# A perceiver block on one core: the matrix work of its first self-attention in another order

## The reference

```python
x = x + cross_attention(ctx_1024, layernorm(x), ...)
x = x + attn(layernorm(x), q_weight, v_weight, out_w, out_b)
x = x + moe_attention(layernorm(x), ...)

def attn(x, q_weight, v_weight, out_w, out_b):     # t = 8, b = 64, 16 heads of 32
    q = einsum('tbm,mhd->tbhd', x, q_weight)
    q_sq = einsum('tbhd,tbhd->tbh', q, q)
    squared_dist = q_sq[:, None] + q_sq[None, :] - 2.0 * einsum('tbhd,sbhd->tsbh', q, q)
    attn_weights = softmax(-squared_dist * inv_sqrt_d, axis=1)
    A = einsum('mhd,nhd->hmn', q_weight, q_weight) * inv_sqrt_d
    XA = einsum('tbm,hmn->tbhn', x, A)
    PXA = einsum('tsbh,sbhm->tbhm', attn_weights, XA)
    PXAV = einsum('tbhm,mhd->tbhd', PXA, v_weight).reshape(...)
    return PXAV @ out_w.T + out_b
```

## Time and profile before

| | us |
|---|---|
| median of 3 runs | 582.81 |
| lowest and highest | 582.78 to 582.81 |
| the profiled execution, whole time | 586.54 |
| its span, first to last instruction | 584.8 |
| TensorE busy in the span | 570.4 |
| VectorE, ScalarE, GpSimd busy | 344.6, 203.7, 222.4 |
| mean granted TensorE clock | 0.991 |

### The profile page before, as it was taken

The page is one execution under the profiler, slowest core; times in us unless marked ns, Lnnn a source line. Parts: engine busy times, 40 slices in busy tenths (PEclk is TensorE's granted clock), DMA queues, the critical chain, the costliest instruction groups (busy, mean ns, idle before and its releaser), DMA issues.

```text
span 584.8 us, 11726 instructions
## 1 busy us (share of the span) xinstructions
PE 570.4 (98%) x5010; PEld 489.0 (84%) x5010; DVE 344.6 (59%) x387; ACT 203.7 (35%) x293; POOL 222.4 (38%) x182
## 2 busy tenths in 40 slices
PE   6999999999999999999999999999999999999997
PEld 6989889898989989897678988988888888788886
DVE  4886871825637082552597446656666345876741
ACT  4444342505335250532652530423342121434320
POOL 2599685564627356461325000202434443000000
PEclk9999999999999999999999978999999999999999
DMA  8764424240322324005210402013923322799701
GB/s 304 280 222 149 154 75 153 72 153 29 114 81 75 149 72 153 1 1 158 61 68 3 154 4 72 17 57 111 245 86 86 130 73 73 156 220 240 176 1 72
DMA packets 25284, 65.76 MB, mean 112 GB/s; under 512 B 2424, under 2 KB 2424, under 8 KB 22304
## 3 DMA queue, kind: packets, MB, share of 16 engines
q1 hardware_dynamic: 25248, 65.23, 36.6%
HBM read 64.05 MB, written 1.18 MB: 112 GB/s over the span
## 4 chain that ended last, share of the span: by engine, by line
PE 90%; DVE 5%; issue 2%; ACT 1%; POOL 1%; DMA 1%; ACTq 0%; DVEq 0%
PE ps L328 17%; PE ps L330 17%; PE ps L329 17%; PE ps L849 10%; PE ps L872 4%; PE ps L876 4%; PE ps L864 2%; PE ps L859 2%; PE ps L863 2%; PE ps L858 2%; PE ps L1148 2%; PE ps L929 1%; PE ps L890 1%; PE ps L897 1%; DVE stats L1358 1%
## 5 line engine op out<-in xcount | busy, mean ns | idle before, releaser
L466 POOL TENSOR_TENSOR psum_tmp<-psum_tmp,raw 128x512 f32<-128x512 f32 (+1 forms) x88 | 140.8, 1600 | 29.4 <-DVE lo L1385 20.7
L849 PE MATMUL ps<-hi 128*128 128x256 f32 (+3 forms) x416 | 130.1, 314 | 5.5 <-ACT hi L543 4.8
L849 PEld LDWEIGHTS ps<-hi 128*128 128x128 f32 (+1 forms) x416 | 79.1, 190 | 6.3 <-ACT hi L543 4.8
L328 PE MATMUL ps<-hi,gh 128*128 128x512 f32 x192 | 75.6, 394 | 1.2 <-DVE gl L1768 1.2
L1385 DVE TENSOR_TENSOR lo<-raw,hi 128x2048 fp32r<-128x2048 f32 (+1 forms) x29 | 63.3, 2215 | 21.4 <-ACT hi L535 21.4
L330 PE MATMUL ps<-hi,gl 128*128 128x512 f32 x192 | 74.8, 390 | 0.0
L329 PE MATMUL ps<-lo,gh 128*128 128x512 f32 x192 | 74.7, 389 | 0.0
L516 POOL TENSOR_TENSOR sx<-sx,raw 128x512 f32<-128x512 f32 x32 | 41.1, 1289 | 78.1 <-DVE raw L1734 78.1
L735 ACT ACTIVATE hi<-raw 128x2048 fp32r<-128x2048 f32 x14 | 26.8, 1917 | 85.5 <-PE ps L330 76.5
L328 PE MATMUL ps<-wvh,gh 128*128 128x512 f32 x128 | 51.1, 399 | 0.2 <-DVE gl L1541 0.2
L330 PE MATMUL ps<-wvh,gl 128*128 128x512 f32 x128 | 50.0, 391 | 0.0
(11 more groups left out here) (224 smaller groups left out, 1177.7 us busy)
## 6 DMA issues: line engine op xcount, KB each, us to landing
raw<-in_ctx SPq DMA_DIRECT2D x23, 1024.0 KB, 4.8
raw<-in_ve SPq DMA_DIRECT2D x8, 1024.0 KB, 5.5
raw<-in_oe SPq DMA_DIRECT2D x8, 1024.0 KB, 7.6
wk<-gm_rows SPq DMA_DIRECT2D x8, 512.0 KB, 9.8
g<-gm_rows SPq DMA_DIRECT2D x8, 512.0 KB, 10.4
raw<-in_ctx SPq DMA_DIRECT2D x8, 130.0 KB
xres<-in_x SPq DMA_DIRECT2D x1, 1024.0 KB, 9.8
mb<-in_WqT SPq DMA_DIRECT2D x1, 1024.0 KB, 13.4
```

The source lines that it names most:

```text
L328: pe.matmul(dst, wh, xh, start=first, stop=False)
L466: pool.tensor_tensor(psum_tmp[0:k, :], (raw[:, 0, :] if t == 1 else psum_tmp[0:k, :]), raw[0:k, t, :], ALU.add).then_inc(ctx_sum, 1)
L849: pe.matmul(dst, hi[0:kk, t, cols], x, start=start and opens, stop=stop and closes, skip_group_check=True)
```

## The change

Nothing is added to the computation or taken from it. The same matmuls, copies and exponentials run in another order, in three PSUM places and partly on another engine:

- TensorE: `half_norms(0)` and `half_norms(1)` come one query block earlier. The fourth query block, `project_1(1, (3,))`, moves from ahead of `distances(0)` to behind it. `distances(1)` moves ahead of `head_values(2)`. `near_values(0)` and `near_values(1)` are cut in two: the halves for groups 0 and 1 stand between `head_values(2)` and `head_values(3)`, the others behind it. `near_values(2)` moves ahead of the first transposes, and `near_values(3)` ahead of all of the projection. The projection finishes tile 0, then 1, 2 and 3, where before the first halves of the tiles 0, 1 and 2 came first.
- Waits: a half of `near_values` waits for the values of its own groups. The wait for the second row terms stands at `near_values(0)` instead of `head_values(3)`, and `head_values(3)` waits for two `vv_done`.
- ScalarE copies out all four groups of values. `w_high(W_Q2, 0, 2)` moves ahead of the third copy, and the split of the gate weights (L704) ahead of `near_high(0)`.
- VectorE: no `values_out`. `near_add(3)` and `w_low(W_Q2, 0)` come ahead of `near_norm(0)`, `near_norm(2)` ahead of `near_low(0)`, and the low part of the gate weights ahead of `near_norm(3)`.
- PSUM: `vv_bank(3)` is bank 7 instead of 0, `num_bank` of the blocks 2 and 3 are exchanged, and `turn_bank` alternates between the banks 0 and 3.

The two copies of values have left VectorE, and the weight split stands ahead of the first division. The diff, cut to what the order doesn't show:

```diff
         def vv_bank(g):
-            return bank[(6, 7, 3, 0)[g]]
+            return bank[(6, 7, 3, 7)[g]]
...
         def num_bank(c, g):
-            return ((0, 3), (6, 7), (1, 2), (4, 5))[c][g // 2]
+            return ((0, 3), (6, 7), (4, 5), (1, 2))[c][g // 2]
...
         def turn_bank(c):
-            return bank[(0, 3, 1, 2)[c]]
+            return bank[3 * (c % 2)]
...
             values_out(1)
+            w_high(W_Q2, 0, 2)
+            values_out(2)
             nearness(2)
             nearness(3)
-            near_high(0)
-            near_high(1)
-            w_high(W_Q2, 0, 2)
+            values_out(3)
...
-                if g >= 2:
-                    pe.wait_ge(row_done, g - 1)
+                if g == 2:
+                    pe.wait_ge(row_done, 1)
+                if g == 3:
+                    pe.wait_ge(vv_done, 2)
...
-            def near_values(c):
+            def near_values(c, gs=range(NG)):
                 pe.wait_ge(d_exp, c + 1)
                 if c == 0:
                     pe.wait_ge(vv_ones, 1)
-                    pe.wait_ge(vv_done, NG)
+                    pe.wait_ge(row_done, 2)
                 if c == 2:
                     pe.wait_ge(d_add, 8)
-                for g in range(NG):
+                for g in gs:
+                    pe.wait_ge(vv_done, g + 1 if c != 1 or g < 2 else NG)
...
             pe.wait_ge(w_lo, 4)
-            near_values(2)
             out_part(0, (0, 1))
-            near_values(3)
-            out_part(1, (0, 1))
             turn_values(2)
             turn_values(3)
-            out_part(2, (0, 1))
-            for i in range(3):
-                out_part(i, (2, 3))
+            out_part(1, (0, 1))
+            out_part(0, (2, 3))
+            out_part(1, (2, 3))
+            out_part(2, range(KC))
             out_part(3, range(KC))
```

More of the change, by code:

```diff
@@ L704, in _ @@
             act.activation(wg_hi, wg_raw, ACT.Copy).then_inc(wg_hi_done, 1)
+            near_high(0)
+            near_high(1)
             near_high(2)
@@ L1096, in _ @@
             transposes_1(3)
-            project_1(1, range(3))
+            project_1(1, range(2))
             half_norms(0)
-            project_1(1, range(3, KC))
+            project_1(1, range(2, 3))
             half_norms(1)
@@ L1150, in near_values @@
                                            vv[row, g, 4 * c + j, :], start=True, stop=True, skip_group_check=True)
-                mm.then_inc(nv_mm, 1)
+                if gs.stop == NG:
+                    mm.then_inc(nv_mm, 1)
             def turn_values(c):
@@ L1161, in _ @@
             distances(0)
+            project_1(1, range(3, KC))
+            half_norms(2)
             head_values(0)
-            half_norms(2)
+            half_norms(3)
             head_values(1)
-            half_norms(3)
+            distances(1)
             head_values(2)
+            near_values(0, range(0, 2))
+            near_values(1, range(0, 2))
             head_values(3)
-            distances(1)
-            near_values(0)
-            near_values(1)
+            near_values(0, range(2, NG))
+            near_values(1, range(2, NG))
+            near_values(2)
             turn_values(0)
             turn_values(1)
+            near_values(3)
             def transpose_e(u):
@@ L1612, in near_add @@
                                       row, ALU.add).then_inc(d_add, 1)
[L1614 to L1618, removed]
             def near_norm(c):
@@ L1637, in _ @@
             row_part(1)
-            values_out(2)
-            values_out(3)
             near_add(2)
+            near_add(3)
+            w_low(W_Q2, 0)
             near_norm(0)
-            near_add(3)
             near_norm(1)
+            near_norm(2)
             near_low(0)
             near_low(1)
-            near_norm(2)
-            w_low(W_Q2, 0)
-            near_norm(3)
             dve.wait_ge(wg_hi_done, 2)
             dve.tensor_tensor(wg_lo, wg_raw, wg_hi.bitcast(F32), ALU.subtract).then_inc(wg_lo_done, 1)
+            near_norm(3)
             near_low(2)
```

## The result

| | before | changed |
|---|---|---|
| median of 20 runs, us | 586.64 | 582.17 |
| lowest to highest | 581.85 to 591.16 | 580.26 to 583.79 |
| ratio to before, 95% interval | | 0.994 (0.9914 to 0.9965) |
| profiled execution, whole and span | 586.54, 584.8 | 580.85, 579.1 |
| mean granted clock of it, as a share of full speed | 0.991 | 1.000 |

The changed kernel is faster by 0.6%. The ratio leaves out runs of a kernel more than 1.5% above its fastest, here four of before (590.8 to 591.2), so it lies nearer to one than the quotient of the two medians, 0.992. The time landed within the predicted range and 0.8 us from the predicted one, but from another base than the one that I used: the three runs of before that were shown (582.8) lay near the lower end of what that kernel does. Between the medians of 20 runs lie 4.5 us, not 1.4.

The account below looks back on a forecast made before the run. TensorE, busy 98% of the span, was taken as the bound. Terms +0.3 + 0.2 - 0.4 - 0.3 - 1.2 = -1.4 us from the median 582.81 give 581.4; likeliest 580.6 to 582.4, whole range 578.0 to 583.9.

Parts of the forecast that it names:

- the fall is the profiled execution's own: Rival: median runs have no clock fall, only waits and tail gain, -0.2 us, 582.6; chance 0.22 including equal loss.
- The clock: TensorE's sparse run from 342.2: fall at start of block 3's products, 3.3 us lost instead of 4.49, -1.2 us.
- the rival of the longer fall: Clock falls at about 344.5, before block 2's products, and stays low into the projection: 5.7 lost, 583.8; chance 0.14.
- Clock stays up: Rival: head values among the products prevent the fall, all of 4.49 us comes back, -4.7, 578.1; chance 0.17.
- Before the first head values: TensorE waits 0.5 us for ScalarE's square of the fourth query block, replacing a 0.22 stall: +0.3, bounds 0 and +0.5.
- The copy of group 3: Block 0's later products: TensorE waits for ScalarE's copy of group 3's values, +0.2 us, bounds 0 to +1.1.
- The second turns: Block 2's products hide the second division, so the 0.43 us wait for VectorE goes: -0.4, up to -0.7.
- The gap before the queries: Next layer's queries: tiles in order free VectorE sooner, gap about 0.7 instead of 0.94 us; -0.3, bounds -0.5 and 0.
- Stalls put down to issue: TensorE durations carried over from the kernel before, among them 3.14 us for the second distances.

Follow-up runs that it names:

- head values together: Changed kernel with the last two blocks of head values together ahead of all value products, these no longer in halves; high-clock median 581.22 us, the others 586.8 to 590.0.
- fourth block first with early turn: Changed kernel with the fourth query block back ahead of the first distances and the next layer's first transposes ahead of the last six projection matmuls; median 580.44 us, ratio 0.9899.
- the kernel with extra matmuls: Kernel before with eight extra 512-column matmuls between the value products of blocks 0 and 1; median of all runs 584.72 us, high-clock median 584.68.
- the tiles in order: Kernel before with only the projection finishing the token tiles in order; high-clock median 583.75 us, the others 586.6 to 591.5.
- block 2 ahead: Kernel before with only block 2's value products moved ahead of the first transposes; high-clock median 583.27 us, the others 585.7 to 592.4.
- extra transposes: Kernel before with 24 extra 128 by 128 transposes between the value products of blocks 0 and 1; high-clock median 584.41 us, the others 586.1 to 588.4.
- turns last: Changed kernel with block 3's value products directly behind block 2's, ahead of the first transposes; median 581.84 us, all 12 runs at high clock.
- third heads first: Changed kernel with the third block of head values ahead of the second distances, as before; high-clock median 581.01 us, the others 583.8 to 584.3.

## Why the prediction held, and where it didn't

**The base.** I subtracted 1.4 us from a median of three runs and arrived at 581.4; measured were 582.17. The three runs agreed within 0.03 us, and I took that for the kernel's spread. It was not: the kernel before has a spread of 9 us, by the clock. My rival "the fall is the profiled execution's own" came near the truth and stopped short of it: those three were presumably executions without a fall (582.8, as the high ones' 582.2), the profiled one had a fall, and over many runs half or more have one. The forecast of the time was right by luck: the base was 3.8 us too low and the gain 3.1 us too small, and the two nearly cancel. Of the change it held the direction and a third of the size.

**The clock.** This is the step that failed. I let the fall come at the start of block 3's products and replaced the 4.49 us of before by 3.3, -1.2, where the profile gives back all of the 4.49. The changed kernel's profile has none, and its runs have rare falls of 0.996 to 0.997. The wrong inference was to measure the sparse stretch from its beginning at 342.2 and carry over the two distances of 4.1 and 7.3 us from one trace. Before, distances and products together stood from 336.8 to 350.7 without head values or projection; in the changed kernel head values stand at 337.4 and at 340.4, and only 7.2 us are left behind them. The fall that I took also counts the first turns ahead of it as part of the sparse stretch; no run shows that transposes weigh in it like products, and with 24 extra ones in it 9 of 12 runs kept the clock, against 9 of 34 without. Nor does a low clock last until the projection in every case, as the rival of the longer fall assumed: it rose at 337.4 (head values together) and at 341.1 (fourth block first with early turn), both in the second distances behind head values. "Clock stays up" had 0.17 and 578.1; from the profiled 586.5 its -4.7 gives 581.8, and 580.85 was measured.

**Waits.** Before the first head values: +0.5 predicted ahead of what it replaced, 0.38 measured. The copy of group 3: +0.2 predicted, 0.21 measured; by the trace ScalarE began it 0.04 behind the head values (341.62 against 341.58), and the weight loads went on 0.05 behind its end (342.27 against 342.22), together the 0.1 that I had estimated for signals. The second turns: wait gone, as predicted, and 0.50 at high clock in the kernel with extra matmuls. The gap before the queries: 0.94 to 0.70, as predicted, and with the tiles alone as well. These four steps were right, within about 0.1 us each. One count in the working is wrong: the rest of blocks 0 and 1 behind the last head values is 64 instructions, not 96; the times given for it are those of 64.

**Stalls put down to issue.** I kept them: I gave the second distances 3.14 us and let the 0.51 among the products stand. In the changed kernel the distances take 2.47 (334.88 to 337.35) and no such stall is left among the products, 1.2 us less than I carried. The waits take off another 0.4 by the traces (+0.16 and +0.21, -0.50 and -0.24). Together that is more than the 0.7 to 1.1 us between the kernels at high clock, and how it divides isn't shown, since no trace of before at high clock is at hand; in other kernels the stall in the distances is 0.17 instead of 0.45. The stalls' cause stays open. The 0.51 stands at the same place in the traces of before, of the tiles in order and of block 2 ahead (after 70 product instructions); extra matmuls between the blocks removed it, extra transposes left 0.21 of it, both left 0.17 in the distances; and ordering the third head values as before did not bring any back.

## What to carry to other kernels

Before pricing a change on a few runs that agree, look at the granted clock of the profile: where it falls once in the middle, the time has a spread that three runs can hide (here 582.78 to 582.81 in the first three, 581.85 to 591.16 in twenty), and the base of the sum may be off by more than the change. Here head values that had to run anyway went into a long stretch of small matmuls, and the clock that stayed up was worth more than the waits that this added (4.5 us in the profiled executions against 0.6); it is the first thing to try where the clock falls in such a stretch. A transpose that feeds another engine can go ahead of the last matmuls of the product before it; here that closed a gap of 0.70 us.

## What the runs showed of the hardware

- The clock can fall in a stretch of small matmuls in which TensorE's gaps are no longer than 0.5 to 0.65 us. Counted from the last head values before it to the next projection matmul, the sparse stretch was 13.8 us in the profiled execution of before (336.8 to 350.7, part of it at low clock; 17 of 35, 25 of 34, 14 of 22 and 10 of 12 runs with a fall), 13.2 and 12.9 us with the tiles in order and with block 2 ahead (8 and 10 of 12), 14.7 us in that of the head values together (341.0 to 355.7; 7 of 12), 8.2 with the turns last (341.3 to 349.5; none of 12) and 7.2 in the changed kernel (341.5 to 348.7; its rare falls are short).
- Two runs of one kernel need not meet the same clock: the same program fell or didn't, and fell for 3.4, 6.8, 10.2, 13.7 or 17 us in the traces at hand.
- Half norms (four moving columns) with a wait of 0.4 to 1.3 us beside them are a second weak place: three traces (head values together, third heads first, fourth block first with early turn) have a fall that begins there; the three traces of the changed kernel have the same wait of 0.4 and none.
- Without any fall the runs still spread by some 3 us. Part of it lies outside the part that was changed: over the traces, the preceding transposes start between 319.0 and 320.9 us, and from the next layer's transposes to the end it takes 218.0 to 219.7. What makes this wasn't looked into.
